# A fused attention and FP4 feed-forward kernel: TensorE turns tile 11 of each batch, and ScalarE's exponentials and VectorE's roundings change places

## The reference

```python
def reference(x, W_Q, W_K, W_V, w_gate, w_up, w_down):
    # attention, all 2048 keys in the softmax, then a decay by distance
    n = layernorm(x)
    Q, K, V = xpos(n @ W_Q), xpos(n @ W_K, downscale=True), n @ W_V
    p = softmax(Q @ K.T) * 0.9 ** abs(i - j)
    x = x + p @ V
    # feed-forward, 704 wide; inputs and weights of each product are
    # quantised to FP4 (E2M1) in blocks of 16 and scaled back
    n = layernorm(x)
    h = silu(fp4(n) @ fp4(w_gate).T) * (fp4(n) @ fp4(w_up).T)
    return x + fp4(h) @ fp4(w_down).T
```

## Time and profile before

| | |
|---|---|
| runs | 2592.87 us median of 3 (2591.42 to 2593.66) |
| profiled execution, its own time | 2587.73 us |
| its span in the profile | 2585.9 us, mean granted TensorE clock 0.989 |
| busy: TensorE, its weight loads | 96%, 86% |
| busy: VectorE, GpSimd, ScalarE | 89%, 74%, 57% |
| chain that ended last, by engine | TensorE 69%, GpSimd 12%, VectorE 9%, issue 6% |

### The profile page before, as it was taken

The page is one execution under the profiler, slowest core; times in us unless marked ns, Lnnn a source line. Parts: engine busy times, 40 slices in busy tenths (PEclk is TensorE's granted clock), DMA queues, the critical chain, the costliest instruction groups (busy, mean ns, idle before and its releaser), DMA issues.

```text
span 2585.9 us, 51840 instructions
## 1 busy us (share of the span) xinstructions
PE 2494.6 (96%) x15392; PEld 2223.9 (86%) x15392; DVE 2304.2 (89%) x5015; ACT 1480.3 (57%) x2966; POOL 1919.5 (74%) x2057
## 2 busy tenths in 40 slices
PE   8999999999999999999999999999999999999996
PEld 7888888888889798988888888978898888888895
DVE  8999889899989898889988998989898998899896
ACT  5766555555556555555655555655565555556553
POOL 6999957777777777767777777767776777777774
PEclk9999999999999999999999999999999999999998
DMA  8878412243222422242224222342224222422222
GB/s 284 297 283 298 180 41 81 75 149 93 86 81 90 152 85 80 86 148 89 84 81 148 90 82 82 93 147 89 79 82 148 90 82 84 148 90 79 85 82 78
DMA packets 255638, 304.00 MB, mean 118 GB/s; under 512 B 25424, under 2 KB 192528, under 8 KB 255376
## 3 DMA queue, kind: packets, MB, share of 16 engines
q1 hardware_dynamic: 255376, 300.72, 35.9%
HBM read 153.75 MB, written 127.93 MB: 109 GB/s over the span
## 4 chain that ended last, share of the span: by engine, by line
PE 69%; POOL 12%; DVE 9%; issue 6%; ACT 2%; DMA 1%; SPq 0%; POOLq 0%; DVEq 0%; ACTq 0%
PE score L555 25%; PE acc L692 15%; PE ring L555 14%; PE acc L555 7%; PE ring L661 6%; POOL q_stage L939 2%; POOL keys L944 2%; DVE h_buf L1113 1%; POOL rot_k L933 1%; DVE hT L1267 1%; DVE h_buf L1116 1%; POOL h_buf L1046 1%; PE acc L721 1%; ACT probs L847 1%; POOL h_buf L1040 1%
## 5 line engine op out<-in xcount | busy, mean ns | idle before, releaser
L555 PE MATMUL score<-keys,q_st 128*128 128x512 f32 x3072 | 742.2, 397 | 3.0 <-ACT probs L847 2.6
L817 ACT ACTIVATE pT<-ring 128x512 fp32r<-128x512 f32 (+3 forms) x432 | 222.9, 529 | 851.5 <-PE ring L661 847.4
L555 PEld LDWEIGHTS score<-keys,q_st 128*128 128x128 f32 x3072 | 573.7, 190 | 119.8 <-issue 3.0
L1025 POOL TENSOR_TENSOR probs<-probs,decay 128x512 f32<-128x512 f32 (+3 forms) x416 | 497.7, 1209 | 145.4 <-ACT probs L847 145.4
L692 PE MATMUL acc<-vals,pT 128*128 128x256 f32 x3984 | 550.4, 287 | 5.8 <-DVE pT L1267 2.1
L555 PE MATMUL ring<-w_gu,xqT 128*128 128x512 f32 (+1 forms) x2304 | 528.8, 378 | 22.9 <-DVE hT L1267 21.3
L692 PEld LDWEIGHTS acc<-vals,pT 128*128 128x128 f32 x3984 | 499.1, 189 | 26.0 <-DVE pT L1267 13.3
L555 PEld LDWEIGHTS ring<-w_gu,xqT 128*128 128x128 f32 x2304 | 413.6, 189 | 111.7 <-DVE hT L1267 51.5
L1280 DVE TENSOR_REDUCE smax<-score 128x1 f32<-128x1024 f32 x256 | 310.9, 1215 | 115.7 <-PE score L555 114.4
L1267 DVE TENSOR_TENSOR pT<-ring,pT 128x512 fp32r<-128x512 f32 (+3 forms) x432 | 248.8, 600 | 50.1 <-ACT pT L817 48.5
L847 ACT ACTIVATE probs<-score,nmax 128x1024 f32<-128x1024 f32 x256 | 284.2, 1128 | 2.0 <-DVE nmax L1283 2.0
(11 more groups left out here) (133 smaller groups left out, 4351.0 us busy)
## 6 DMA issues: line engine op xcount, KB each, us to landing
h_dram<-hq_buf SPq DMA_DIRECT2D x128, 384.0 KB, 2.3
h_moved<-h_dram SPq DMA_DIRECT2D x512, 96.0 KB, 2.2
k_dram<-keys SPq DMA_DIRECT2D x56, 512.0 KB, 4.6
keys<-k_dram SPq DMA_DIRECT2D x56, 512.0 KB, 6.8
edge<-vals SPq DMA_DIRECT2D x288, 64.0 KB, 2.0
q_raw<-q_dram SPq DMA_DIRECT2D x129, 128.0 KB, 2.6
x_in<-X SPq DMA_DIRECT2D x32, 512.0 KB, 4.6
q_dram<-q_stage SPq DMA_DIRECT2D x32, 512.0 KB, 5.3
```

Source lines behind the costliest of these rows:

```text
L555: mm = pe.matmul(dst, stat(a, k), mov(m, k), start=i == 0, stop=ends and i == n - 1)
L817: act.activation(dst, src, ACT.Copy).then_inc(hi_done, 1)
L1025: op = pool.tensor_tensor(probs[:, k0:k1], probs[:, k0:k1], decay[:, off + k0:off + k1], ALU.mult)
```

## The change

1. Tile 11 of every batch, and tiles 13, 14 and 15 of the last batch, are not moved through DRAM (`on_tensor`). GpSimd writes their `hq` in natural order (five instructions for three), TensorE turns them in six transposes in the step of their down product, after the last group but one (`later`), and SyncE and VectorE leave them out. `moved_before` counts the moved tiles for the semaphores.
2. ScalarE's exponentials are split: the first half follows xqT's upper part, then group 3, both halves of hT, then the second half and the sum.
3. VectorE turns both halves of hT after xqT's lower part in every step, and writes both lower parts before the levels in every step.
4. GpSimd's subtraction becomes a function of its own, called at the same place. The plan of the ring lists hT after all groups, which gives the same order as before.

```diff
+ON_TENSOR = (11,)
+        def on_tensor(at, t):
+            return t % T in ON_TENSOR or at[2] is end_plan and t >= T - 3
+        def moved_before(j, t, step=1):
+            per = [u % T not in ON_TENSOR and (t - u) % step == 0 for u in range(-T, T)]
+            return j * sum(per[T:]) + (sum(per[T:T + t]) if t >= 0 else -sum(per[T + t:T]))
...
 SyncE, rows_moved:
+                if t % T in ON_TENSOR:
+                    return
-                sp.wait_ge(h_out, (g + 1) * 16)
+                sp.wait_ge(h_out, (moved_before(j, t) + 1) * 16)
...
-                if s - MOVED < T:
+                if s - MOVED < T - 3:
...
 TensorE, attend:
                     if g == 0:
                         meanwhile()
+                    if g == max(len(gs) - 2, 0):
+                        later()
+
+            def h_transposed(at, t):
+                if has(at, t) and on_tensor(at, t):
+                    pe.wait_ge(hq_ready, tile(at, t) + 1)
+                    for h, ks in enumerate((range(0, CT), range(CT, HK))):
+                        dst = slot(at, "hT", t, h)
+                        for j, k in enumerate(ks):
+                            mm = pe.transpose(dst[:, j * P:(j + 1) * P], hq[t % 2][:, k * P:(k + 1) * P], ident[:])
+                        mm.then_inc(h_turned, 1)
...
-                attend(at, s - 1, lambda: x_transposed(at, s - 2))
+                attend(at, s - 1, lambda: x_transposed(at, s - 2), lambda: h_transposed(at, s - LAG))
...
 ScalarE, step:
                 x_transposed(at, s - 2)
+                if s < T and not begins:
+                    exponentials(at, s, 0)
                 attend(at, s - 1, range(3, n))
-                if n <= 3:
-                    h_transposed(at, s - LAG, 0)
+                h_transposed(at, s - LAG, 0)
+                h_transposed(at, s - LAG, 1)
                 if s < T and not begins:
-                    exponentials(at, s)
-                if n > 3:
-                    h_transposed(at, s - LAG, 0)
-                h_transposed(at, s - LAG, 1)
+                    exponentials(at, s, 1)
...
 GpSimd, h_quantised:
+                    if on_tensor(at, t):
+                        whole = q.rearrange("p (n c i) -> p n c i", c=CT, i=QUAD)
...
+                        for c in range(CT):
...
+                        op.then_inc(hq_ready, 1)
+                        return
...
 VectorE, step:
                 attend(at, s - 1, range(min(n, 2)))
-                h_turned_blocks(at, s - LAG, "begun")
                 maxima(at, s, 1)
...
                 x_transposed(at, s - 2)
-                h_turned_blocks(at, s - LAG, "x")
+                h_turned_blocks(at, s - LAG)
                 attend(at, s - 1, range(3, n))
-                h_turned_blocks(at, s - LAG, "all")
-                if n <= 3:
-                    h_transposed(at, s - LAG, 0)
+                h_transposed(at, s - LAG, 0)
+                h_transposed(at, s - LAG, 1)
                 h_levels(at, s - 3)
-                if n > 3:
-                    h_transposed(at, s - LAG, 0)
-                h_transposed(at, s - LAG, 1)
                 residual(at, s - 1)
```

More of the change, by code:

```diff
@@ L46 @@
 RING = 3
-XR, LAG, LATER = 8, 5, 3
+XR, LAG = 8, 5
 MOVED, QUAD = 4, 32
+ON_TENSOR = (11,)
 W_SLOTS = 3
@@ L126, in step @@
                 take("xqT", s - 2)
+        if has(s - LAG):
             for h in range(2):
-                if g == min(max(len(gs) - LATER, 0) + h, max(len(gs), 1) - 1) and has(s - LAG):
-                    take("hT", s - LAG, h)
+                take("hT", s - LAG, h)
         if has(s - 2):
@@ L667, in attend_begun, with attend @@
                     group(at, t, 1)
-            def attend(at, t, meanwhile):
+            def attend(at, t, meanwhile, later):
                 if not has(at, t):
                     meanwhile()
+                    later()
                     return
@@ L839, in h_transposed, with exponentials @@
                         act.activation(hT[0][:, h * CT:h * CT + n, :].rearrange("p k t -> p (k t)"), bank(at, "hT", t, h)[:, 0:n * P], ACT.Copy).then_inc(hi_done, 1)
-            def exponentials(at, s):
+            def exponentials(at, s, h):
                 g = tile(at, s)
[L843 to L852, removed]
+                if h == 0:
+                    if s == 0 and at[2] is first_plan:
+                        act.wait_ge(rot_added, 2 * NCH)
+                    act.wait_ge(nmax_set, g + 1)
+                act.activation(probs[:, h * 2 * CH:(h + 1) * 2 * CH].rearrange("p (j n) -> p j n", j=2),
+                               score[:, 2 * h:2 * h + 2, :], ACT.Exp, bias=nmax[:, s % 2:s % 2 + 1],
+                               accum_out=psum_row[:, s % 2, h:h + 1]).then_inc(exped, 1)
+                if h:
+                    act.wait_ge(exped, 2 * g + 2)
+                    act.activation(rsum[:, s % 2:s % 2 + 1], psum_row[:, s % 2, 0:1], ACT.Identity,
+                                   bias=psum_row[:, s % 2, 1:2]).then_inc(summed, 1)
             def x_centred_rows(at, t):
@@ L1040, in h_scaled, with h_levelled_rows @@
                     pool.tensor_tensor(blocks(hv[t % 2]), blocks(hv[t % 2]), spread(hrs[:], HB), ALU.mult).then_inc(hv_ready, 1)
+            def h_levelled_rows(at, t):
+                if has(at, t):
+                    pool.wait_ge(hg_ready, tile(at, t) + 1)
+                    pool.tensor_tensor(hv[t % 2], hv[t % 2], he[t % 2], ALU.subtract).then_inc(h_levelled, 1)
             def h_quantised(at, t):
@@ L1299, in h_transposed, with h_turned_blocks @@
                         lower(lo, bank(at, "hT", t, h)[:, 0:n * P], hi, at, "hT", t, h)
[L1301 to L1305, removed]
+            def h_turned_blocks(at, t):
+                if has(at, t) and not on_tensor(at, t):
+                    for h, (k0, k1) in enumerate(((0, CT), (CT, HK))):
+                        dve.wait_ge(h_back[t % 2], (moved_before(at[0], t, 2) + 1) * CT * 16)
                         dve.wait_ge(freed, nth(at, "hT", t, h) - (RING - 1) + PRIME)
-                        k0, k1 = (0, CT) if h == 0 else (CT, HK)
                         dve.transpose(bank(at, "hT", t, h)[:, 0:(k1 - k0) * P].rearrange("p (k a j) -> p k a j", a=CT, j=QUAD),
                                       h_moved[t % 2][:, :, k0 * QUAD:k1 * QUAD].rearrange("p a (k i) -> p k a i", i=QUAD)).then_inc(h_turned, 1)
-            def turn_place(at, t, h):
-                n = len(groups((t + LAG - 1) % T))
-                return ("begun", "x") [h] if n <= 3 else ("x", "all")[h]
             def residual(at, t):
```

20 lines of the change are left out of this document (14 added, 6 removed).

## The result

The changed kernel takes 2649.64 us (median of 4 runs, 2646.08 to 2651.62); the kernel before took 2593.26 us beside it. The ratio is 1.022, with a 95% interval of 1.0207 to 1.0232: **slower by 56 us**, where I had forecast slower by 28 (2621) and a range up to 2637. The profiled execution took 2646.08 us, with a span of 2644.2 for 2585.9.

A forecast was written before the change was run, and what follows sets the result against it. TensorE, busy 96% of the span, was taken as the bound. New waits and transposes, less old hT waits, gave 38.6 us over seven batches; with first batch, ends and tail +28 on 2592.9: 2621 us, range 2560 to 2637.

The forecast's parts named there:

- TensorE's transposes: Step 0 of each batch: six more transposes for tile 11 at 0.11 us each, 0.66 a batch; 0.7 in the tail.
- GpSimd and VectorE beside it: nothing: Step 0: GpSimd's write in five instructions for three costs nothing; the two turns VectorE saves buy nothing.
- SyncE free: Batch ends: v_raw and edge rows go out some 9 us sooner; -3.7 us at the first end, other waits stay.
- Waits for hT gone: Gate and up products: TensorE's waits for VectorE's lower parts go, 3.95 us a batch, -27.6 over seven batches.
- The meeting: VectorE's later level instructions meet GpSimd's first weightings; in step 3 the reciprocal comes 1.05 plus 1.85 us later.
- Who waits for that: TensorE's next probability transposes wait for the gate and up products' second bank, freed after the reciprocal: 8.8 us a batch.
- Step 15 hidden by the loop end: Batch end: the lateness in step 15 is hidden by TensorE's loop-end wait, whose 4.34 us stay.
- The tail: End of the last batch: tiles 13 to 15 skip two transfers each, -5 us (bounds -9 and 0), plus 0.7 of transposes.
- The sum: Whole kernel: 7 x (8.8 - 3.95 + 0.66) = 38.6 us, with first batch, ends and tail +28 in all.
- The third: Rival: in steps 6 to 13 too VectorE's lateness adds up, 9.5 us a batch, 2650 us; chance 0.08.
- The first two: Rivals: levels miss the weightings, 2563 us, chance 0.26; VectorE wins the tie, one weighting waited for, 2579 us, chance 0.12.

The follow-up runs named there:

- the fastest version: The changed kernel with VectorE's residual ahead of the levels and the turn back in its places of before: 2527.06 us, ratio 0.9752.

## Why the prediction was wrong, point by point

- **TensorE's transposes**: right in themselves. They add 0.57 us a batch (0.66 in the sum) at 0.11 apiece. The Trainium skill ("TensorE: Matmul & The Clock Gate", Part 4) puts one at about 275 ns in a kernel's context; the trace has this as the length of a single one (0.27 us), not as the distance of two in a row. "GpSimd and VectorE beside it: nothing" was not right in the order of before: tile 11 alone cost 18 us, 15 of them by a new meeting in step 1. In the changed kernel steps 0 and 1 are long anyhow.
- **SyncE free**: right. Step 0 behind the first batch is 2.4 us shorter where the other steps 0 are 1.5 longer, so this end gave 3.9; I had 3.7. The six waits at the loop ends stayed (28.2 us for 25.8).
- **Waits for hT gone**: right. Steps 6, 7 and 9 to 11 are shorter by 0.26 to 0.43 each. Step 8 is 0.21 longer: steps 6 and 8 have 0.5 and 0.4 us more ahead of the gate products, which the sum had at 0.4 for steps 6 to 11 in all.
- **The meeting**: right in place and size. In step 3 I had the reciprocal 2.90 us later; it comes 2.82 later (14.49 for 11.67 after the step's first score product).
- **Who waits for that**: the step that failed. I let TensorE be held only at the next step's probability transposes by the bank of the gate and up products. It is held ahead of the down product, by the residual; ahead of the transposes there is no new wait (0.58 to 0.91 us from the down product to the next scores in steps 0 to 14, as before). In the kernel before, the residual ended 0.5 to 1.3 us ahead of the down product in the steps with three groups (12.34 for 13.50 in step 3), and some 0.15 of that is the way from the one to the other. In step 3 that slack is near the 1.3 us that I had counted to the bank, so its wait came out nearly right by luck (1.64 for 1.6). In others it is much shorter than what I had. Steps 4 and 5 wait 1.9 and 1.1 (1.3 and 0.6 in the sum), and steps 0, 12 and 13, for which I had 0.1 in all, are 1.5 (0.57 of it the transposes), 0.7 and 0.6 longer. Behind each such wait the down product takes 0.1 more, which the sum lacked. In all the new waits are 13.3 us a batch for 8.8: the change of steps 0 to 14 (9.7), plus 4.1 of old waits that are gone, less 0.5 of transposes.
- **Step 15 hidden by the loop end**: wrong. The step is 0.8 longer, and the wait behind it did not shrink by that: it is 4.77 us for 4.34, so what ends it came later too. My reading that it ends just after the DMA engines have drained does not hold: their busy share falls from 0.80 to 0.10 at 855.0, 2.5 us ahead of TensorE's next product, and in the fastest version TensorE goes on at 845.83 while the share is still over 0.8. The DMA records point at something else. At all 84 loop ends of the fourteen kernels TensorE goes on 1.8 to 2.2 us after a 16 KB packet of the kind "instruction" has landed (855.73 for 857.56 in the kernel before, 861.25 for 863.15 in the changed one), while the waits themselves are from 0.9 to 4.8 us long. So the wait looks like a fetch of instructions behind the loop's jump. What makes the packet earlier or later is not shown, and no run was made on it.
- **The tail**: 9.4 us shorter for 4.3. Alone, in the old order, it is 4.8 shorter in the trace, near what I had; the rest came with the new order of the lower parts and with the clock, which the sum did not have.
- **The sum**: 7 x 10.5 in place of 7 x 5.5 is +35; the tail is -5 against the forecast: +58 in place of +28. The tail's and the end's terms only shift it by a few us; the waits decide.
- **The rivals.** The third, VectorE as the bound everywhere, has the time (2650) but not the mechanism: steps 6, 7 and 9 to 11 became shorter, not longer. The first two hung on whether the levels miss the weightings or meet one; in step 3 they meet two, and the third level instruction is held for over 0.6 us in 92 of the 128 tiles.
- One reading of the kernel before was also wrong: I took the first batch for the only place where the meeting can be seen. It was there in step 2 of every batch, and with it the row that prices it beside the work of TensorE:

```profile
899.38 1.04 DVE L1113 TENSOR_SCALAR h_buf<-h_buf 128x704 int32<-128x704 int32 x1 [0.21 <-POOL h_buf L1040]
...
900.21 2.34 POOL L1025 TENSOR_TENSOR probs<-probs,decay 128x256 f32<-128x256 f32 x2 [0.17 <-ACT probs L847]
900.46 0.95 DVE L1116 TENSOR_SCALAR h_buf<-h_buf 128x704 f32<-128x704 f32 x1
901.44 1.86 DVE L1120 SCALAR_TENSOR_TENSOR h_buf<-h_buf 128x704 f32<-128x704 f32 x1
...
903.56 0.15 DVE L1322 RECIPROCAL rinv<-rsum 128x1 f32<-128x1 f32 x1
```

That is why step 2, alone of steps 0 to 5, did not get longer: its meeting was already paid for.

## What to carry to other kernels

When an instruction moves later on one engine, list every wait of the others for what stands behind it, and take the slack of each from the trace, step by step: the first wait in program order with the least slack decides, not the one you found first. Where two engines hold each other up, look for work that does not take part (here the residual and the statistics) and put that beside the other engine's work; here this one line turned 2.2% slower into 1.2% faster, a part of it at the loop ends. Measure a change of several parts part by part, and in the order in which it is to stand: tile 11 on TensorE cost 18 us in the old order and gained 17 in the best one.

## What the runs showed of the hardware

- Two weightings of 384 columns take 2.54 us beside the levels in step 3 of the changed kernel, two times 1.0 alone, and the third level instruction goes from 0.89 to 1.85: one is held for the length of the other's. The Trainium skill ("SBUF — State Buffer", "SBUF: two separate sides") calls the pair of ports that VectorE and GpSimd share a lock that one side has for its whole instruction, and counts among VectorE's holders those with two SBUF inputs or in a mode with two ports. The trace agrees in length, and also in who stays out: in the run with the residual first, statistics over 256 columns take 0.43 us in the midst of a weighting (915.78). The residual, one of whose inputs lies in PSUM, takes 0.48 in all 128 tiles of the kernel before, in 108 of them with a weighting under way, as in step 3 beside the earlier trace rows:

```profile
919.22 0.48 DVE L1327 SCALAR_TENSOR_TENSOR x_res<-acc,rinv,x_res 128x256 f32<-128x256 f32 x1
```

- Of two that wait, the order in the traces is one by one: in step 3 each of the second and third level instruction waited for one weighting, never for both.
- A down product that starts behind a wait takes 1.78 to 1.85 us from its first to its 16th product, one that does not 1.72.
